# Layer norms: the inverse root by a power on GpSimd instead of ScalarE's root and VectorE's reciprocal

## What is computed

```python
def _layernorm(x, axis=-1, eps=1e-05):
    m = jnp.mean(x, axis=axis, keepdims=True)
    v = jnp.var(x, axis=axis, keepdims=True)
    return (x - m) / jnp.sqrt(v + eps)

x = x + _L0_xattn_ref(ctx_1024, _layernorm(x), ...)
x = x + _L0_ffn_ref(_layernorm(x), ...)      # 8 experts
x = x + _L1_xattn_ref(_layernorm(x), ctx_1024, ...)
x = x + _L1_ffn_ref(_layernorm(x), ...)      # self-attention, then 8 experts
x = x + _L2_xattn_ref(_layernorm(x), ctx_1024, ...)
x = x + _L2_ffn_ref(_layernorm(x), ...)      # 8 experts
x = x + _L3_xattn_ref(_layernorm(x), ctx_1024, ...)
x = x + _L3_ffn_ref(_layernorm(x), ...)      # fp4 weights
```

## Time and profile before

| | us |
|---|---|
| median of 3 runs | 2608.32 |
| lowest, highest | 2603.58, 2614.10 |
| the profiled execution | 2606.42 |
| its span | 2604.7 |

### The profile page before, as it was taken

The page is one execution under the profiler, slowest core; times in us unless marked ns, Lnnn a source line. Parts: engine busy times, 40 slices in busy tenths (PEclk is TensorE's granted clock), DMA queues, the critical chain, the costliest instruction groups (busy, mean ns, idle before and its releaser), DMA issues. The chain is left out here.

```text
span 2604.7 us, 36305 instructions
## 1 busy us (share of the span) xinstructions
PE 2169.0 (83%) x12226; PEld 1294.6 (50%) x12227; DVE 1298.5 (50%) x2489; ACT 1071.6 (41%) x2187; POOL 649.1 (25%) x569
## 2 busy tenths in 40 slices
PE   6899999981967975999998499994967999777786
PEld 3333333351853541333334399993347999632554
DVE  5655545257046458888863400004561440265885
ACT  4434444430322620777775244442633444325111
POOL 1228888931430060000000122220002222120011
PEclk9999999995987985999999599997988999878898
DMA  2000000011630035225320756653046666400000
GB/s 66 5 1 9 14 13 14 22 62 53 210 113 1 21 129 65 34 34 62 38 34 1 253 192 199 200 180 90 1 163 233 201 199 199 134 13 1 1 1 33
DMA packets 141679, 214.34 MB, mean 82 GB/s; under 512 B 39649, under 2 KB 97693, under 8 KB 141549
## 3 DMA queue, kind: packets, MB, share of 16 engines
q1 hardware_dynamic: 131276, 186.10, 26.1%
q0 software_dynamic: 9696, 26.49, 2.7%
q10 hardware_dynamic: 576, 0.07, 0.0%
HBM read 182.00 MB, written 30.15 MB: 81 GB/s over the span
## 5 line engine op out<-in xcount | busy, mean ns | idle before, releaser
L2883 PE MATMUL experts_up_ps<-experts_rowT,experts_w 128*128 128x128 f32 x2864 | 341.7, 278 | 0.0
L2883 PEld LDWEIGHTS experts_up_ps<-experts_rowT,experts_w 128*128 128x128 f32 x2864 | 333.6, 195 | 0.2
L1833 ACT ACTIVATE heads_probs<-heads_score_ps 128x512 f32<-128x512 f32 x512 | 267.8, 603 | 153.0 <-PE heads_score_ps L1773 153.0
L1849 DVE TENSOR_REDUCE heads_part_max<-heads_shared_ps 128x2 f32<-128x1024 f32 x256 | 300.0, 1220 | 53.8 <-PE heads_shared_ps L1751 52.9
L3043 DVE TENSOR_TENSOR experts_y<-experts_down_ps,experts_b_now 128x256 f32<-128x256 f32 x78 | 33.1, 425 | 499.4 <-PE experts_down_ps L2893 499.2
L1343 POOL TENSOR_TENSOR core_xT<-core_xT,heads_probs 128x1024 f32<-128x1024 f32 (+1 forms) x112 | 263.9, 2356 | 25.2 <-ACT heads_probs L1516 11.8
L2951 ACT ACTIVATE experts_hT<-experts_up_ps,experts_b_now 128x128 f32<-128x128 f32 x624 | 207.7, 367 | 86.6 <-PE experts_up_ps L2883 69.4
L1555 DVE TENSOR_REDUCE heads_part_max<-heads_shared_ps 128x1 f32<-128x512 f32 x256 | 164.4, 686 | 147.1 <-PE heads_shared_ps L1385 146.9
L2832 POOL DMA_INDIRECT y_dram<-experts_y,experts_index x101 | 99.4, 984 | 456.1 <-DVE experts_y L3043 411.3
L1516 ACT ACTIVATE heads_probs<-heads_score_ps 128x1024 f32<-128x1024 f32 x128 | 131.0, 1023 | 177.8 <-PE heads_score_ps L1412 177.8
L1773 PE MATMUL heads_score_ps<-heads_q,heads_k 66*128 66x512 f32 x512 | 187.8, 448 | 4.0 <-ACT heads_probs L1833 4.0
(11 more groups left out here) (565 smaller groups left out, 3234.7 us busy)
## 6 DMA issues: line engine op xcount, KB each, us to landing
experts_w<-in_L_ffn_W SPq DMA_DIRECT2D x39, 1024.0 KB, 4.6
experts_w<-in_L_ffn_w SPq DMA_DIRECT2D x39, 1024.0 KB
experts_w<-in_L_ffn_W SPq DMA_DIRECT2D x23, 512.0 KB
experts_w<-y_dram SPq DMA_DIRECT2D x20, 512.0 KB, 8.3
experts_b_now<-in_L_ffn_b SPq DMA_DIRECT2D x78, 128.0 KB
heads_q<-l_queries SPq DMA_DIRECT2D x32, 256.0 KB, 11.8
heads_k<-l_keys SPq DMA_DIRECT2D x32, 256.0 KB, 13.5
l1f_w<-in_L_ffn_W SPq DMA_DIRECT2D x8, 1024.0 KB, 9.7
```

Of the source, the lines that this page charges most:

```text
L1833: act.activation(probs[:, t % SLOTS_OF_PROBS, r, :], score_ps[:, i % RING, :], ACT.Exp, scale=SC).then_inc(exp_done, 1)
L1849: dve.tensor_reduce(part_max[:, g % 2, 2 * pair:2 * pair + 2, s, x], two, AX.X, ALU.max).then_inc(shared_read, 1)
L2883: done = pe.matmul(up_ps[:, f % 4, 0:SLOT], w1_sb[:, u, c, f * P:(f + 1) * P], rowT[:, u % 2, c, :], start=(c == 0), stop=(c == DC - 1))
```

## The change

The factor 1/sqrt(variance + eps) of 128x16 is no longer made by ScalarE's root and VectorE's reciprocal, but on GpSimd, by a scale with an addition and then a power with the exponent -0.5, which stands in a tile of its own. In the two double norms the same is done for the second factor. The call of a root for its table goes, and with it the tile of eps.

```diff
+        exponent = st.sb("exponent", [P, NT])
-        eps, warm = st.sb("eps", [P, 1]), st.sb("warm", [P, 1])
-        eps_done, warmed = st.sem("eps_done"), st.sem("warmed")
+        shifted = st.sem("shifted")
...
-            dve.memset(eps[:], LN_EPS).then_inc(eps_done, 1)
...
             dve.wait_ge(std_done, 1)
-            done(dve.reciprocal(rstd[:], std[:]))
             dve.wait_ge(moments, n)
...
                 dve.wait_ge(root_done, 1)
-                done(dve.reciprocal(second[:], std[:]))
-                dve.wait_ge(moments, n)
                 done(dve.tensor_tensor(second[:], second[:], rstd[:], ALU.mult))
...
+        @block.gpsimd
+        def _(pool):
+            pool.memset(exponent[:], -0.5).then_inc(shifted, 1)
+            pool.wait_ge(var_done, 1)
+            pool.tensor_scalar(std[:], var[:], 1.0 / D, LN_EPS, ALU.mult, ALU.add).then_inc(shifted, 1)
+            pool.wait_ge(shifted, 2)
+            pool.tensor_tensor(rstd[:], std[:], exponent[:], ALU.pow).then_inc(std_done, 1)
+            if second_eps is not None:
+                pool.wait_ge(spread_done, 1)
+                pool.tensor_scalar(std[:], second[:], 1.0 / D, LN_EPS, ALU.mult, ALU.add).then_inc(shifted, 1)
+                pool.wait_ge(shifted, 3)
+                pool.tensor_tensor(second[:], std[:], exponent[:], ALU.pow).then_inc(root_done, 1)
+
         @block.scalar
         def _(act):
-            act.wait_ge(eps_done, 1)
-
-
-            act.activation(warm[:], eps[:], ACT.Sqrt).then_inc(warmed, 1)
-            act.wait_ge(var_done, 1)
-            act.activation(std[:], var[:], ACT.Sqrt, scale=1.0 / D, bias=eps[:, 0:1]).then_inc(std_done, 1)
-            if second_eps is not None:
-                act.wait_ge(spread_done, 1)
-                act.activation(std[:], second[:], ACT.Sqrt, scale=1.0 / D, bias=eps[:, 0:1]).then_inc(root_done, 1)
```

## The result

The changed kernel takes 2636.47 us (median of 5 runs, 2631.16 to 2642.96) against 2608.32 before (2603.58 to 2614.10): 1.0109 times as long, 95% interval 1.0086 to 1.0132. That is 28.2 us slower. The forecast was 2612.8 and the range ended at 2633, so the time lies above both. The profiled execution took 2637.23 us.

The account below looks back on a forecast made before the run. Each norm's serial head, from variance to first normalisation, was taken to bound its stage. Seven loaded chains +2.1, ln0f +0.8 and two second chains +1.6 gave +4.5 us on 2608.32: 2612.8 us, range 2601 to 2633.

Parts of the forecast that it names:

- p: Duration of one GpSimd power of 128x16 in the norms, taken as 1.0 us by likeness to the indirect DMA.
- 11p - 7.2: Forecast change of the whole time in us for p beyond 1.64, where ln2f's cover is gone too.
- the cover: At ln2f's end SyncE's issue of a weight load ends the stage, so 1.43 us of delay is free.
- the multiplicity: 11 chains from variance to inverse: seven with a table load, ln0f and ln2f, and second ones in ln0x and ln1f.
- 64 additions to a power: Upper estimate of the power of 16 columns: as long as the 1024-column addition, 2.36 us.
- the dear power: Rival: a long GpSimd routine holds VectorE at L246 eleven times; at p = 2.36 +18.8 us, 2627; chance 0.20.
- The handovers: In each chain, all but the power: handover to GpSimd, tensor_scalar, GpSimd's own wait and way back, 0.45 us.
- the four of the exponential: Exponential table loads at L1833, L922, L674 in x3 and L925 in gate2 go; costed at nothing, hidden before waits.
- those of the norms: Root-table loads in seven of nine norms, 1.28 us long, held back each chain by 0.48 us.
- the load in or behind ln0x: Root table loaded once in ln0x or the projection behind; in the projection hidden in ScalarE's 2.92 us wait.
- the drain of 1380 ns: Skill page's extra cost per table switch, some 10 us more for seven; the prediction took the trace, which shows none.
- The clock: Rival: shifts move stages between granted clock levels, 1.7 us for one gate, perhaps 5 us together; lucky clock chance 0.03.

Follow-up runs that it names:

- the product: Changed kernel with each power replaced by a product of the same shape, all factors 0.5: 2604.91 us against 2610.71 for the kernel before, ratio 0.9975.
- the kernel with early loads: Kernel before, roots kept, with a root of a constant called at the end of stages ahead of norms: 2613.65 us against 2607.77, ratio 1.0026.
- the two pairs of executions: Kernel before and changed kernel, each profiled once, then each executed once more unchanged: the second pair took 2615.86 and 2630.84 us.

## Why the prediction was wrong

**The term that failed is p.** The sum took 1.0 us for a power of 128x16; it took 2.90 to 2.94 in the norms. Its own formula, 11p - 7.2, gives +24.9 at 2.92; ln0x's table load makes 26.2, and the nine norms grew by 26.0. So the path, the cover and the multiplicity were right, and the size of one term was off threefold. The upper bound failed too: 2.36 us came from "64 additions to a power" over a fixed 0.18 us, and measured are 75 additions' worth a column over a fixed 0.35. Taking 1.0 us because the indirect DMA is the only other long routine on GpSimd was an argument by likeness between things that have nothing in common but their engine: all that is shown of the power is that it goes by its columns, and no run shows of what steps it consists. The text gave the dear power 0.20 and said that nothing bounds the routine; then the range should not have ended 6 us past a bound that was only invented. Its end, 2633, is the sum at p = 2.9, the value that came. The median went 3.5 us past it: 1.3 us are ln0x's table load, and some 2 us lie outside the norms.

**The handovers were right.** 0.45 us was put for all but the power; 0.42 was measured, with 0.10 to GpSimd, 0.20 for the tensor_scalar, 0.08 in between and 0.04 on the way back. With the product of 0.22 us the chain was 0.64 for a predicted 0.66.

**Where the loss counts was right.** ln2f was forecast to lose 1.43 us less than the others since SyncE ends that stage; it grew by 1.25 us where its chain grew by 2.7. ln1g lost in full, and gained nothing when its chain was shortened (12.94 us with the product, 11.54 with the table loaded early).

**The table loads were half right.** That the four of the exponential were hidden is borne out by putting them back, and that those of the norms held back 0.48 us each by the kernel with early loads, whose chain in ln1x is 0.67 us instead of 1.15. The step that put the load in or behind ln0x at nothing failed in ln0x. The prediction looked for cover only for a load in the projection, and named none for one in ln0x; the load at L285 had started with the stage. The new one starts only when the first copy is released, behind the transposes. Why it stands behind its instruction's wait, where those of gate1, gate2 and x3 ran ahead of one, no run here shows. On the drain of 1380 ns that the Trainium skill (ScalarE: Activation LUTs, "What ACT_TABLE_LOAD costs") adds to a switch, the trace was rightly preferred: with loads out and in, no norm and no gate but ln0x differs by more than 0.1 us from both executions of the changed kernel, and there it is 1.30 us. Nor is there a gap in front of a load that stands right behind work: in gate2 of before ScalarE's instruction in front of the load ends at 1934.61, and the load starts at 1934.63.

**Of the rivals** the dear power happened. The clock was priced at some 5 us, and x2 alone moved 9.8 us between two executions of one program; the price was too low. It did not decide: outside the norms the two pairs of executions differ by +4.4 and -11.2 us, and the norms by 26.0 and 25.8.

## What to carry to other kernels

A power on GpSimd is paid by the column (0.160 us each), so ask how many columns it has and what waits for it. Against a root and a reciprocal on ScalarE and VectorE, which take 0.67 us for the same tile with the table there, the power can't win on a serial head at 16 columns. Taking table loads away is worth only what they hold back after the work beside them, and whoever takes the first away has to look at which instruction inherits it.

## What was not expected of the hardware

- The power on GpSimd: 0.160 us a column over 0.35 us, the same for 16, 64 and 128 partitions and for exponents -0.5, 1 and 2.
- A table load at the head of a waiting instruction: in ln0x it ran behind the wait (22.02, released by TensorE), elsewhere ahead of it.
- Two executions of one program differed by 9.8 us in one stage (x2), at a granted clock of 1.00 and 0.89.
- A GpSimd product of 128x256 took 4.54 us beside a VectorE addition of 4.43 us, where its columns account for some 0.7.
